# A cross-attention and MLP kernel: weight rings of four and six tiles with one load per tick, a layer norm spread over two ticks, a drain by chunks, and GpSimd making two low parts of four

## The reference

```python
# L0, of which only batch 0's attention is used
q, k, v = x @ Wq.T, ctx @ Wk.T, ctx @ Wv.T
att     = softmax(q k^T / sqrt(32)) v
x       = x + att[0]                      # att[0] is added to all 8 sequences
# L1, for each of the 8 sequences
xq, ykv = layer_norm(x) * gq + bq, layer_norm(ctx) * gkv + bkv
q, k, v = xq @ Wq, ykv @ Wk, ykv @ Wv
o       = softmax(q k^T / sqrt(32)) v
x       = x + o @ Wproj + bproj
h       = layer_norm(x) * gm + bm
x       = x + gelu(h @ W1 + b1) @ W2 + b2  # 512 -> 2048 -> 512
```

## Time and profile before

| | |
|---|---|
| median of three runs | 1991.66 us |
| the profiled execution | 2001.36 us, of which the span from first to last instruction 1999.4 us |
| PE busy | 1796.6 us (90%), 7488 matmuls |
| DVE, ACT busy | 1165.2 us (58%), 1165.1 us (58%) |
| POOL busy | 749.9 us (38%), 625 instructions |
| mean granted TensorE clock | 0.949 of full speed |
| moved by DMA | 354.67 MB, 177 GB/s on the mean |

### The profile page before, as it was taken

One profiled execution on the slowest core, in us unless ns is written; L12 is line 12 of the kernel. 1 busy time (PEld: TensorE's weight loads), 2 busy tenths in 40 slices (PEclk: granted clock), 3 DMA queues, 4 the chain that ended last, 5 costly groups with the idle time before them and its releaser, 6 DMA issues.

```text
span 1999.4 us, 23652 instructions
## 1 busy us (share of the span) xinstructions
PE 1796.6 (90%) x7488; PEld 1361.1 (68%) x7488; DVE 1165.2 (58%) x2004; ACT 1165.1 (58%) x1922; POOL 749.9 (38%) x625
## 2 busy tenths in 40 slices
PE   7899898989978989989999899899899989999888
PEld 5677676766655766767666677667676767667676
DVE  4566564678856646655665576467556555663322
ACT  3767664678856647654755575466547654764120
POOL 0355421345534334333434343343334343343221
PEclk9999999999989989999999899899999999999898
DMA  6699964556626644654465456536645554555233
GB/s 230 231 319 356 353 212 148 199 189 202 209 87 166 174 144 119 201 165 131 140 177 169 119 165 201 168 96 198 199 125 148 168 169 137 146 163 190 105 134 140
DMA packets 156379, 354.67 MB, mean 177 GB/s; under 512 B 28512, under 2 KB 47072, under 8 KB 155360
## 3 DMA queue, kind: packets, MB, share of 16 engines
q1 hardware_dynamic: 119392, 218.92, 35.6%
q10 hardware_dynamic: 36864, 134.23, 20.9%
HBM read 251.51 MB, written 82.08 MB: 167 GB/s over the span
## 4 chain that ended last, share of the span: by engine, by line
PE 56%; DMA 10%; ACT 9%; issue 8%; SPq 6%; POOL 5%; DVE 5%; ACTq 0%; DVEq 0%; POOLq 0%
PE ps_d L802 39%; PE ps_o L851 8%; DMA w_r<-w_scratch 6%; PE ps_t L834 4%; PE ps_s L819 4%; DMA q_st<-negmax_t 3%; SPq L591 2%; SPq L596 2%; ACT ps_t L955 2%; POOL p_lo L1196 1%; ACT p_hi L949 1%; PE ps_d L732 1%; ACT ps_d L867 1%; DVE negmax L1089 1%; ACT ht L925 1%
## 5 line engine op out<-in xcount | busy, mean ns | idle before, releaser
L949 ACT ACTIVATE p_hi<-ps_t 128x512 fp32r<-128x512 f32 x576 | 345.1, 599 | 524.0 <-PE ps_t L834 521.8
L1102 DVE TENSOR_TENSOR p_lo<-ps_t,p_hi 128x512 fp32r<-128x512 f32 x432 | 297.5, 689 | 338.9 <-ACT ps_t L955 336.5
L802 PE MATMUL ps_d<-w_r,g_s 128*128 128x512 f32 x1536 | 419.4, 412 | 42.7 <-DMA w_r<-w_scratch 42.7
L1196 POOL TENSOR_TENSOR p_lo<-p_full,p_hi 128x512 fp32r<-128x512 f32 x144 | 185.8, 1290 | 698.2 <-ACT p_full L955 698.0
L802 PE MATMUL ps_d<-hT,w_r 128*128 128x512 f32 x1536 | 432.1, 399 | 7.2 <-DMA w_r<-w_scratch 6.5
L1089 DVE TENSOR_REDUCE negmax<-ps_s 128x1 fp32r<-128x512 f32 x576 | 388.7, 677 | 80.0 <-PE ps_s L819 79.8
L802 PEld LDWEIGHTS ps_d<-w_r,g_s 128*128 128x128 f32 x1536 | 305.9, 200 | 124.8 <-DMA w_r<-w_scratch 47.1
L802 PEld LDWEIGHTS ps_d<-hT,w_r 128*128 128x128 f32 x1536 | 293.7, 192 | 85.2 <-issue 7.3
L834 PE MATMUL ps_t<-q_st,k_st 97*128 97x512 f32 x576 | 240.6, 418 | 52.0 <-DMA q_st<-negmax_t 31.4
L955 ACT ACTIVATE ps_t<-ps_t 128x512 f32<-128x512 f32 x432 | 257.9, 597 | 0.0
L851 PE MATMUL ps_o<-p_hi,v_s 128*65 128x512 f32 x576 | 237.9, 413 | 18.3 <-ACT o_raw L969 15.4
(11 more groups left out here) (98 smaller groups left out, 2189.7 us busy)
## 6 DMA issues: line engine op xcount, KB each, us to landing
w_r<-w_scratch ACTq DMA_DIRECT2D x256, 512.0 KB, 5.2
v_scratch<-v_out SPq DMA_DIRECT2D x36, 520.0 KB, 4.2
v_s<-v_scratch SPq DMA_DIRECT2D x36, 520.0 KB, 3.7
k_scratch<-kq_out SPq DMA_DIRECT2D x36, 512.0 KB, 5.3
q_scratch<-kq_out SPq DMA_DIRECT2D x36, 512.0 KB, 3.0
q_st<-q_scratch SPq DMA_DIRECT2D x144, 128.0 KB, 3.5
k_st<-k_scratch SPq DMA_DIRECT2D x144, 128.0 KB, 3.9
o_ab<-o_raw SPq DMA_DIRECT2D x144, 128.0 KB, 3.1
```

The costliest lines, as they stand in the source:

```text
L802: ins = nc.tensor.matmul(bank(u), lhs[a], rhs[b], start=(i == 0 and m == 0), stop=(i == 3 and m == 2))
L949: act.activation(p_hi[:, c], ps_t[:, c % 2], ACT.Exp, scale=SCALE)
L1102: dve.tensor_tensor(p_lo[:, c], ps_t[:, c % 2], p_hi[:, c].bitcast(F32), ALU.subtract).then_inc(p_split, 1)
L1196: pool.tensor_tensor(p_lo[:, POOL_CHUNK], p_full[:], p_hi[:, POOL_CHUNK].bitcast(F32), ALU.subtract).then_inc(p_pool_split, 1)
```

## The change

It touches seven things.

- **Weight rings.** `w1_r` stays a ring of 4; `w2_r` becomes a ring of 6 tiles, loaded tile by tile. `weight_tables` gives each load a tick of its own: a W1 tile six ticks ahead of its `hid`, a W2 tile 12 to 6 ticks ahead of its group's first `y2`, never before its place in the ring is free. In the drain the loads are issued by SP, not by ACT. `h_st`, where Gelu works, shrinks from two buffers to one to make room.
- **GpSimd's chunks.** `POOL_CHUNKS = (0, 2)`: POOL makes `p_lo` of chunks 0 and 2, DVE of 1 and 3. `p_full` gets two buffers.
- **Projection and norm.** `out` waits for each of its four parts apart, and comes one tick later; the last `hid` parts ahead of it are packed tighter. For all passes the scaling comes one tick after the root. The burst behind it moves from tick 23 to 24; the other three are at 5, 40 and 55.
- **Gap.** Eight ticks, with four of the remaining key and value units put between the first three transposes `tg` and the last one.
- **Pieces.** Those of W1 stay in pass 0, one in five ticks; those of W2 move to pass 1, ticks 4 to 39 after `base[1]`. The split of Wproj moves to tick 48 and is cut in four, the sum with the bias is cut in four.
- **Queries.** The last six units of the queries move from before the projection of pass 2 to ticks 22 to 34 behind it.
- **Drain.** `y2` of sequence 7 is spread between the steps of the norm; Gelu is made a chunk at a time.

```diff
-POOL_CHUNK = 2
+POOL_CHUNKS = (0, 2)
...
-        for i, units in enumerate(([("tg", 0, g) for g in range(G - 1)] + late[:8], [("tg", 0, G - 1)],
-                                   late[8:11], late[11:14],
+        for i, units in enumerate(([("tg", 0, g) for g in range(G - 1)] + late[:2], late[2:6], [("tg", 0, G - 1)],
+                                   late[6:11], late[11:14],
...
-        spread(range(base[1], base[2] + 14), queries[:-2])
+        spread(range(base[1], base[2] + 15), queries[:-6])
...
             if old:
                 burst(at + 5, old, 2, second(old, 1)[:2])
-                spread(range(at + 6, at + 14), second(old, 1)[2:] + hidden(old, 3)[:2])
-                spread(range(at + 14, at + 23), outs + hidden(old, 3)[2:])
-                burst(at + 23, old, 3, second(old, 2)[:2])
+                spread(range(at + 6, at + 15), second(old, 1)[2:] + hidden(old, 3)[:3])
+                spread(range(at + 15, at + 22), outs)
+                spread(range(at + 22, at + 24), hidden(old, 3)[3:])
+                burst(at + 24, old, 3, second(old, 2)[:2])
...
-    at = [emptied("out", i, t) for t in range(TC)]
-    if i < NP - 1:
-        at = [t + 1 for t in at]
-    return tuple(at), at[-1], (at[-1],) * 4
+    at = tuple(emptied("out", i, t) for t in range(TC))
+    return at, at[-1], (at[-1] + 1,) * 4
...
+W1_RING, W2_RING = 4, 6
...
+            u = freed_by(kind, j)
+            freed = PLAN.end(*u) + 1 if u else 0
+            if kind == "w1":
+                at = PLAN.starts["hid", n, c] - 6
+            else:
+                at = PLAN.starts["y2", n, c // 4 * 4] - 12 + 2 * (c % 4)
+            at = max(freed, at)
+            if at < PLAN.base[NP]:
+                early.append((at, (kind, j)))
+            else:
+                late.append((NO[u], PLAN.end(*u), (kind, j)))
...
-                if c == 0 and i == 0:
-                    pe.wait_ge(o_joined, (n + 1) * G)
+                if c == 0:
+                    pe.wait_ge(o_joined, n * G + i + 1)
...
                 if t == 0:
-                    if i == 0:
-                        pe.wait_ge(g_split, done + 1)
-                    pe.wait_ge(w2_loaded[i], 16 * ((n - 1) * 4 + group + 1))
+                    pe.wait_ge(g_lo, 4 * done + i + 1)
+                    pe.wait_ge(w2_loaded[j % W2_RING], 16 * (j // W2_RING + 1))
...
-                if c % 4 == 0 and done >= 2:
-                    dve.wait_ge(g_split, done - 1)
+                if done:
+                    dve.wait_ge(g_lo, 4 * done - 3 + c % 4)
```

More of the change, by code:

```diff
@@ L135, in build @@
         self.gap = gap
-        self.base = {n: gap + 7 + (n - 1) * CH for n in range(1, NP + 1)}
+        self.base = {n: gap + 8 + (n - 1) * CH for n in range(1, NP + 1)}
         self.core(CH, NP * CH, self.base[1])
@@ L349, in sync_tables @@
     for n in range(1, NP):
[L350 to L360 removed]
+        res.append((PLAN.base[n + 1] - (40 if n == 1 else 0), n))
         if n < NP - 1:
@@ L704, in _ @@
                 load_residual(n)
+            for kind, j in LATE_W_LOADS.get(tick, []):
+                load_weight(kind, j)
             for n, t in OUT_STORES.get(tick, []):
@@ L959, in _ @@
                 done = GELU_NO[n, group]
-                if c == 0:
-                    act.wait_ge(gelu_done, done + 1)
-                act.activation(g_s[:, done % 2, 0, c], h_st[:, done % 2, c], ACT.Identity).then_inc(g_hi, 1)
+                if (n, group) in PLAN.by_chunk.get(tick, []):
+                    act.wait_ge(evacuated, ready("hid", n, 4 * group + c))
+                    act.activation(h_st[:, c], h_st[:, c], ACT.Gelu).then_inc(gelu_done, 1)
+                act.wait_ge(gelu_done, 4 * done + c + 1)
+                act.activation(g_s[:, done % 2, 0, c], h_st[:, c], ACT.Identity).then_inc(g_hi, 1)
             s = PLAN.pv_at.get(tick)
@@ L1237, in _ @@
                                    ALU.add).then_inc(b2_summed, 1)
-            if tick == WO_AT:
-                split_wo()
+            for c in range(FC):
+                if tick == WO_AT + 2 * c:
+                    split_wo(c)
     block_cm.__exit__(None, None, None)
```

276 lines of the change are left out of this document (154 added, 122 removed).

## The result

The changed kernel takes **1889.13 us** at the median of four runs (1884.11 to 1890.59), the kernel before 1991.58 beside it. The ratio is 0.9475, 95% interval 0.9452 to 0.9499. It is 102.5 us faster. The forecast was 142 and a time of 1850, with a range of 1818 to 1893: sign and range hold, the gain was forecast 39% too high, and the time lies outside the forecast's own case of 1828 to 1870. The question of this study is which terms of the sum fell short.

A forecast was written before the change was run, and what follows sets the result against it. PE was taken as the bound everywhere. Gains of 92 (passes 3 to 8), 17, 14 and 19 make 142, off the profiled 2001.36: 1859; that execution lay 9.7 above the median, so 1850 us, range 1818 to 1893.

The forecast's parts named there:

- the forecast's own case: Whole kernel: the prediction's terms hold and no rival does; 1828 to 1870 us, chance 0.63.
- Weight tiles: Passes 3 to 8: all 34.0 us of PE's waits for weight tiles go, since loads are issued further ahead.
- Join: Passes 3 to 8, ahead of `out`: all 19.3 us of waits for the join's last step on POOL go.
- Norm and Gelu: Burst at tick 24, passes 3 to 8: PE waits 2.7 us for `o_raw`, before 3.5; 16 us over six passes.
- Row of maxima: Near the end of passes 3 to 8: waits for the row loaded into `q_st` go from 15.0 to 12 us.
- Clock at 0.65 us for each us waited: Passes 3 to 8: each us PE waits loses 0.65 us of clock; 18 us of clock left after the change.
- GpSimd at nothing: All passes: `p_lo` moved to POOL costs nothing while it has two ticks, 4.7 us, of cover.
- The first and fourth rivals: First: GpSimd's `p_lo` comes late, 1882 us, chance 0.12. Fourth: GpSimd bounds every pass, slower, 2018 us, chance 0.03.
- Passes 1 and 2: Gain 17 us: pass 2 gains 20 from waits and clock, pass 1 loses 3 to pieces holding back `p_lo`.
- Pass 0 and gap: Gain 14 us: 8 from the gap's wait with its clock, 6 from half the pieces leaving pass 0.
- Drain: Gain 19 us, bounds 8 and 28: idle 14 in place of 27, two tile waits of 3.8 each left.
- Second rival: Transfers are the limit, not their place: row's wait doubles, a third of tiles' wait stays; 1893 us, chance 0.12.

The follow-up runs named there:

- the late store: The changed kernel with the 1 MB store of a finished sequence issued four ticks later, at tick 50 instead of 46: 1854.74 us.
- the ring of four: The changed kernel with the W2 weight ring at 4 places again instead of 6, loads keeping the changed spacing: 1916.89 us.
- the pairs of kernels: Kernels without and with all weight pieces back in pass 0: the changed kernel 1889.13 and 1883.43 us; with the store four ticks later 1854.74 and 1857.81.

## Why the prediction was right, and which terms were off

**How right it was.** The sign was right, and in passes 3 to 8, where two thirds of the gain lie, the mechanism was too. That the range holds is in good part luck. The 1889 lies 19 us above the forecast's own case and between the centres of the first two rivals, 1882 and 1893, for whose sake the range was drawn so wide, and neither of them is what happened. Of the 39.5 us that were missing, 19 are in passes 3 to 8 and 23 in passes 1 and 2; gap, pass 0 and drain gave 12 more than forecast. The other 9 are in no stretch: the sum took off all of the 9.7 us by which the profiled execution lay above the median before, as if the one after would lie as far above its own median, and that one lay 0.8 above.

Of the signs that I had named, there is no row for `w_r` or `oT`, the wait for `o_raw` at the burst is 2.88, and POOL is at 935.6. But passes 3 to 8 take 170.4 to 175.7 us, only two of them within 168 to 172 and one above the 175 that I had called a sign of being wrong; DVE has 71 us less and not 99; and the drain's two waits for tiles are of 2.4 us and not of 3 to 4.

**Passes 3 to 8, 73 in place of 92.** PE's busy time at full clock in them is 972 us (five times 162.4 and 160.1, from the late store's passes at 1.00); I had 966. After the change they hold 47 of idle time and 21 of clock on top, where I had 37 (28 and 9) and 18. So 6 of the 19 us are the work's own size, 10 idle time, 3 clock.

- *Weight tiles, 34.0 to 0*: right, no row is left. That the tiles' landing stays (5.0 median, 9.2 longest, beside the earlier trace rows) is as assumed. Why it worked I had half: the ring of four kept them away too. And its price in time, 34 with its clock, was not the tiles' alone: undone by itself it costs 12.5.
- *Join, 19.3 to 0*: right. I had needed both the later tick and the waits part by part; either alone is enough.
- *Norm and Gelu, 2.7 at the burst*: measured 2.88 six times, 17.3 in place of 16. The step that failed here is the list of what stands behind: a second wait of 1.46 in each pass at tick 29, 8.7 us, where ACT has the copies of `g_s` and the evacuations into `hT` ahead of `o_raw`. I had counted ACT's queue only through the burst.
- *Row of maxima, 12*: 16.0 measured. I named the store at tick 46 among its causes and took it as one of many. Moving it alone takes 14.8 of the 16.0 away; the tiles beside it are the other half of the cause, since the ring of four, with the store in its place, doubles the wait.
- *Clock at 0.65 us for each us waited*: with 972 us at full clock it was 0.56 before (51 on 91) and is 0.45 after the change (21 on 47), so the mean was too high from the start; as a price for one wait it was wrong. The row's 14.8 us had another 14.8 with them, the burst's and the norm's some 2 either way.

**GpSimd at nothing**: right. POOL is busy 935.6 us, as forecast, and undoing the move changes nothing. The first and fourth rivals fall with it: PE has no wait for POOL's `p_lo` in passes 3 to 8, and 2.6 and 2.1 us of it in passes 1 and 2.

**Passes 1 and 2, 17 forecast, -5.8 measured.** This is the term with the wrong sign. The step that failed is the price of the pieces in pass 1: I had 3 us, as POOL's time, and they cost 14 to 18. When they leave pass 1 again (164.6 to 147.0 us), three things go. The waits for the row of maxima fall by 8.2, beside a DMA share that falls from 0.76 to 0.59. PE's busy time falls by 5.9, which is clock. And 5.6 us of other waits go, those for POOL's `p_lo` (2.6 to none) and those for `negmax` (6.5 to 3.5). Here POOL's time did count: the longest wait for `negmax` in the changed kernel begins with a piece, which stands on POOL ahead of a sum that DVE needs, and `negmax` comes behind that on DVE:

```profile
451.76 2.42 POOL L1195 TENSOR_TENSOR piece_out<-w_raw,piece_out 128x1024 fp32r<-128x1024 f32 x1
...
455.44 1.29 DVE L1104 BATCH_NORM_STATS2 stats<-stage 128x6 f32<-128x512 f32 x2 [3.87 <-POOL stage L1278]
...
457.37 0.62 PE L879 MATMUL ps_s<-k_st,q_st 96*128 96x512 f32 x1 [2.97 <-DVE negmax L1147]
```

It is not the load of `p_lo` on POOL: with one chunk on GpSimd pass 1 still takes 162.1, and the seven other kernels with the pieces in pass 1 take 159.9 to 162.1. By these the changed kernel's own 164.6 is some 3 us long for no reason that was found.

I also overlooked that some 40 matmuls, 9 us, move from pass 1 to pass 2 (592 to 554, 583 to 624 records). That changes nothing in the sum, but at equal work pass 1 lost some 19 where I had 3, and pass 2 gained 14 of the 20. Two stalls in pass 2 took part of it, for which nothing was run: 3.66 us at tick 25, where ACT has the scaling ahead of `o_raw`, and 5.75 right behind the burst at tick 44, which has no matmuls as fill (before, 2.89 for `p_lo` and 0.66 for `o_raw` stood there).

```profile
574.04 0.69 PE L911 MATMUL ps_o<-p_hi,v_s 128*65 128x512 f32 x1 [3.66 <-ACT o_raw L1029]
...
626.73 0.69 PE L911 MATMUL ps_o<-p_hi,v_s 128*65 128x512 f32 x1 [5.75 <-ACT o_raw L1029]
```

**Pass 0 and gap, 14 forecast, 19.7 measured.** The gap gave 6.8 of the 8 that I had for it, pass 0 gave 12.9. Half the pieces leaving gave 10 to 17 in the pairs of kernels, not 6, which is the other side of pass 1's loss: in sum the split of the pieces over two passes is worth nothing that these runs can tell.

**Drain, 19 forecast, 25.1 measured.** Idle time went from 27.3 to 12.1 (I had 14). The two waits for the last tiles of a group are there, at 2.4 us each where I had 3.8:

```profile
PE ps_d L862 <- DMA w_r<-w_scratch: 5.5, 4, 2.4
```

The rest, 9.9 us, is clock (0.91 to 0.98). The forecast of 19 did not follow from its own parts: 13 us less idle time at 1.65 make 22. With four places the drain has 8.1 and 8.8 us of tile waits and takes 5 to 7 us more, so here the ring's size does seem to serve the tiles.

**Second rival.** Its mechanism was at work: the transfers crowd around tick 46, the DMA share is 0.95 to 1.05 for 18 us of pass 5, and the row's wait is 16 us (it had 30). But the tiles' wait is gone (it had 11), and the limit holds for that stretch and not for the pass: the same bytes with the store four ticks later take 34 us less. That its total of 1893 is near the measured one is chance.

## What to carry to other kernels

When a small load comes late, look at what every queue has under way around it, and not only at what its own queue issued ahead of it. Here a 1 MB store among weight tiles made a head's loads land in 8 us in place of 5, and moving it to where no tile stands beside it gave 31 us in six passes, although it still stands ahead of a head's loads. Edits that each remove the same waits don't add, so undo each alone before crediting it. And when work is moved into a stretch, count its transfers, what stands behind it on its engine, and the matmuls that move with it, not only the busy time of the engine that does it.
